# A four-layer gated cross-attention kernel: scales folded into the second weights on GpSimd, the last attention tile's normalization moved into the last stage

## The reference, cut to what matters

```python
x = x + tanh(g_xattn[0]) * L0_xattn(layernorm(x), ctx, ctx)        # stage A
x = x + tanh(g_ffn[0])   * L0_ffn(layernorm(x), ...)               # stage B
x = x + tanh(g_xattn[1]) * L1_xattn(layernorm(x), ctx, ...)        # queries, attention (C)
x = x + tanh(g_ffn[1])   * L1_ffn(layernorm(x), ...)               # stage D, causal attention
# L0_ffn, its end:
x = silu(x_gate) * x_up
x = fwht(x * SU_dp) / SCALE
x = x @ W_down.T * (Wscale_dp * SCALE)
```

## Time and profile before

| | |
|---|---|
| median of three runs | 2069.22 us (2066.19, 2069.22, 2069.27) |
| the profiled execution | 2064.52 us, its span 2062.8 us, mean granted TensorE clock 0.988 |
| TensorE busy | 1998.7 us (97%), weight loads 1677.0 us (81%) |
| VectorE busy | 1238.1 us (60%) |
| ScalarE busy | 1158.9 us (56%) |
| GpSimd busy | 826.3 us (40%) |
| DMA | 210.08 MB, mean 102 GB/s |

### The profile page before, as it was taken

How to read it: one execution, slowest core, us unless ns; L and a number is a source line. 1 busy time by engine, 2 the same in 40 slices (tenths; PEclk the granted TensorE clock), 3 DMA queues, 4 the chain that set the end, 5 groups by cost and what they waited for, 6 DMA issues and landing times. The chain is left out here.

```text
span 2062.8 us, 37477 instructions
## 1 busy us (share of the span) xinstructions
PE 1998.7 (97%) x13369; PEld 1677.0 (81%) x13369; DVE 1238.1 (60%) x2346; ACT 1158.9 (56%) x3064; POOL 826.3 (40%) x997
## 2 busy tenths in 40 slices
PE   8999999999999999999979998899999999899998
PEld 6877777777778888898868886799999999778886
DVE  6666666666644544564445555666666666466665
ACT  6666666666643333353333445877777777355544
POOL 3526436445321000000003445888888878022222
PEclk9999999999999999999989998999999999999999
DMA  6536346454364110203003434333333332311001
GB/s 185 155 93 193 121 132 206 119 154 140 104 246 166 62 61 1 72 1 118 1 26 107 122 117 148 91 95 98 115 100 110 93 112 88 116 59 54 28 28 37
DMA packets 193272, 210.08 MB, mean 102 GB/s; under 512 B 59533, under 2 KB 133757, under 8 KB 192589
## 3 DMA queue, kind: packets, MB, share of 16 engines
q1 hardware_dynamic: 193101, 207.83, 32.9%
HBM read 128.13 MB, written 79.66 MB: 101 GB/s over the span
## 5 line engine op out<-in xcount | busy, mean ns | idle before, releaser
L1864 POOL TENSOR_TENSOR qd_rows<-qd_rows,c_rsum 112x375 f32<-112x375 f32 x256 | 202.2, 811 | 85.5 <-DVE c_rsum L1994 78.3
L2000 DVE TENSOR_TENSOR c_pT_lo<-c_turned,c_pT_hi 125x336 fp32r<-125x336 f32 x256 | 128.4, 502 | 131.5 <-ACT c_pT_hi L1939 131.5
L1930 ACT ACTIVATE qd_rows<-c_score,c_nmax 112x375 f32<-112x375 f32 x256 | 147.1, 574 | 86.7 <-DVE c_nmax L1989 86.7
L1291 ACT ACTIVATE b_silu<-b_gate,ab_scales 128x512 f32<-128x512 f32 (+1 forms) x64 | 40.7, 636 | 252.8 <-PE b_up L1422 252.8
L1355 DVE SCALAR_TENSOR_TENSOR b_hidden<-b_up,ab_scales,b_silu 128x512 f32<-128x512 f32 (+1 forms) x64 | 43.7, 683 | 202.3 <-ACT b_silu L1291 202.3
L531 ACT ACTIVATE a_probs<-a_score,a_nmax 112x375 f32<-112x375 f32 x256 | 144.5, 575 | 2.6 <-DVE a_nmax L700 2.6
L2278 POOL TENSOR_TENSOR f_probs<-f_probs,f_rsum 112x448 f32<-112x448 f32 x64 | 59.7, 933 | 212.4 <-DVE f_rsum L2399 212.4
L953 PEld LDWEIGHTS a_turned<-keep_ident,a_probs 112*125 112x125 f32 x768 | 110.2, 188 | 35.4 <-issue 22.5
L1989 DVE TENSOR_REDUCE c_nmax<-c_score 112x1 f32<-112x375 f32 x256 | 137.4, 537 | 0.4 <-PE c_score L2070 0.4
L953 PE MATMUL a_turned<-keep_ident,a_probs 112*125 112x112 f32 x768 | 133.7, 283 | 1.0 <-DVE a_pT L706 0.7
L1269 POOL TENSOR_TENSOR ab_zT<-ab_zT,keep_ln_eps 128x1 f32<-128x1 f32 x1 | 0.2, 189 | 310.5 <-DVE ab_zT L1389 310.5
(11 more groups left out here) (347 smaller groups left out, 6074.7 us busy)
## 6 DMA issues: line engine op xcount, KB each, us to landing
q<-q_qT SPq DMA_DIRECT2D x14, 1024.0 KB
qd_raws<-q SPq DMA_DIRECT2D x64, 224.0 KB, 4.2
k<-bq_raw SPq DMA_DIRECT2D x16, 752.0 KB, 4.1
qd_raws<-k SPq DMA_DIRECT2D x64, 188.0 KB, 3.0
v<-bq_raw SPq DMA_DIRECT2D x48, 250.0 KB
qd_raws<-v SPq DMA_DIRECT2D x64, 187.5 KB
bq_raw<-in_ctx_dram SPq DMA_DIRECT2D x15, 672.0 KB
wug<-a_ug_turned SPq DMA_DIRECT2D x32, 256.0 KB, 2.3
```

What stands on the lines that cost most here:

```text
L1864: pool.tensor_tensor(probs[:, n % AHEAD, :], probs[:, n % AHEAD, :], rsum[:, n % (2 * H):n % (2 * H) + 1].broadcast_to([S, T]), ALU.mult). ...
L1930: act.activation(probs[:, n % AHEAD, :], score[n % AHEAD][0:S, 0:T], ACT.Exp, bias=nmax[:, c:c + 1], accum_out=sums[:, c:c + 1]).then_inc( ...
L2000: dve.tensor_tensor(pT[1][:, t % 2, :, j, :], src, f32(pT[0][:, t % 2, :, j, :]), ALU.subtract).then_inc(pT_split, 1)
```

## The change

It does three things.

First, `down_scale` is no longer multiplied into y. GpSimd multiplies it into each chunk's second weights in place, once, during the first group; ScalarE waits for it before it makes the chunk's high part in that group. The order on GpSimd is written out: chunks 0 and 1 before the addition L1251, chunk 2 after the deviation, 3 to 9 after the rotation, 10 to 15 after the head scales.

Second, statistics, deviation, normalize and the store of xn3 of the attention's last tile are done in the last stage. The two-tile buffers of both stages become one memory (`cd`), so that the tile stays where it is; the semaphores of the stores are handed over, and SP's wait for the stores moves to the last stage, in front of the loads of x3 and of later sequences.

Third, a projection of the last stage waits for the low part of x3 only before its second pass, and for the high part before its first.

```diff
@@ phase_b @@
         @block.gpsimd
         def _(pool):
+            def scale_down(c):
+                if c >= LEAD:
+                    pool.wait_ge(w_loaded[c], 32)
+                pool.tensor_tensor(down_chunk(c), down_chunk(c), down_scale[:, :], ALU.mult).then_inc(down_scaled, 1)
+
+            pool.wait_ge(scale_done, 1)
+            for c in range(LEAD):
+                scale_down(c)
             pool.wait_ge(ab["xres_loaded"], 16 * B)
...
+            scale_down(2)
             pool.wait_ge(z_done, 1)
...
+            for c in range(3, 10):
+                scale_down(c)
             pool.wait_ge(head_loaded, 32)
...
             pool.tensor_tensor(head_scale, head_clip, half, ALU.pow).then_inc(head_scaled, 1)
+            for c in range(10, IC):
+                scale_down(c)
...
+                if g == 0:
+                    act.wait_ge(down_scaled, c + 1)
                 act.activation(wd[0][:, p, :], down_chunk(c), ACT.Copy).then_inc(wd_hi, 1)
...
                     for k in range(TILES[g]):
                         dve.wait_ge(y_ready, first_tile[g] + k + 1)
-                        dve.tensor_tensor(y[k][:, :], y[k][:, :], down_scale[:, :], ALU.mult).then_inc(y_scaled, 1)
-                    for k in range(TILES[g]):
-                        dve.wait_ge(y_scaled, first_tile[g] + k + 1)
                         dve.tensor_tensor(xio[:, k, :], y[k][:, :], xio[:, k, :], ALU.add).then_inc(x_done, 1)
@@ phase_c_attention @@
-        xout = m.sb("xout", [P, 2, D])
-        xnorm = m.sb("xnorm", [P, 2, D])
+        xout, xnorm = cd["xout"], cd["xnorm"]
...
                 sp.dma_start(by_tiles(io["x3"])[i, :, :], xout[:, i % 2, :]).then_inc(x_stored[i % 2], 16)
+                if i == TILES - 1:
+                    return
                 sp.wait_ge(n_done, i + 1)
...
-            for i in range(2):
-                sp.wait_ge(x_stored[i], 16 * (TILES // 2))
-                sp.wait_ge(n_stored[i], 16 * (TILES // 2))
...
-                if i is not None:
+                if i is not None and i < TILES - 1:
                     deviations(i)
...
-                if i is not None:
+                if i is not None and i < TILES - 1:
                     moments(i)
...
-                if i is not None:
+                if i is not None and i < TILES - 1:
                     normalize(i)
@@ phase_d @@
-        xin = m.sb("xin", [S, 2, D])
-        xout = m.sb("xout", [S, 2, D])
+        xin, xout = cd["xnorm"][0:S, :, :], cd["xout"][0:S, :, :]
...
             load_weight("p")
+            sp.wait_ge(n_done, 1)
+            sp.dma_start(io["xn3"].rearrange("b s d -> (b s) d").rearrange("(t p) d -> t p d", p=P)[last_tile, :, :], tile_norm).then_inc(qd["n3_stored"][last_tile % 2], 16)
+            for i in range(2):
+                sp.wait_ge(qd["x3_stored"][i], 16 * (B * S // P // 2))
+                sp.wait_ge(qd["n3_stored"][i], 16 * (B * S // P // 2))
             for b in range(2):
                 load_residual(b)
...
+                if t == 1:
+                    pool.wait_ge(x_moments, 1)
+                    pool.tensor_tensor(x_ve[:, :], x_mv[:, 1:2], keep["ln_eps"][:, :], ALU.add).then_inc(x_shifted, 1)
+                    pool.wait_ge(x_shifted, 1)
+                    pool.tensor_tensor(x_rstd[:, :], x_ve[:, :], keep["neghalf"][:, 0:1], ALU.pow).then_inc(x_scaled, 1)
...
             weights_lo("v")
+            dve.bn_stats(x_bn[:, :], tile_out).then_inc(x_counted, 1)
+            dve.wait_ge(x_counted, 1)
+            dve.bn_aggr(x_mv[:, :], x_bn[:, :]).then_inc(x_moments, 1)
             for u in range(SLOTS + 3):
...
                 if u < WP_PARTS:
                     output_weights_lo(u)
+                if u == 0:
+                    dve.wait_ge(x_scaled, 1)
+                    dve.tensor_scalar(tile_norm, tile_out, x_mv[:, 0:1], x_rstd[:, 0:1], ALU.subtract, ALU.mult).then_inc(n_done, 1)
...
-                pe.wait_ge(work_lo, split_number(g, "x3"))
+                pe.wait_ge(work_hi, number(g, "x3"))
...
                 for m_, (s, r) in enumerate(PASSES):
+                    if m_ == 1:
+                        pe.wait_ge(work_lo, split_number(g, "x3"))
```

More of the change, by code:

```diff
@@ L1135, in phase_b @@
         xt_loaded = [m.sem(f"xt_loaded{g}") for g in range(GROUPS)]
-        x_loaded, x_done, y_ready, y_scaled = (m.sem(n) for n in ("x_loaded", "x_done", "y_ready", "y_scaled"))
+        x_loaded, x_done, y_ready, down_scaled = (m.sem(n) for n in ("x_loaded", "x_done", "y_ready", "down_scaled"))
         x_stored = bq["x2_stored"]
@@ L1398, in _ @@
                     dve.wait_ge(x_loaded, 16 * g + 16)
-                    dve.wait_ge(scale_done, 1)
                     for k in range(TILES[g]):
                         dve.wait_ge(y_ready, first_tile[g] + k + 1)
-                        dve.tensor_tensor(y[k][:, :], y[k][:, :], down_scale[:, :], ALU.mult).then_inc(y_scaled, 1)
-                    for k in range(TILES[g]):
-                        dve.wait_ge(y_scaled, first_tile[g] + k + 1)
                         dve.tensor_tensor(xio[:, k, :], y[k][:, :], xio[:, k, :], ALU.add).then_inc(x_done, 1)
@@ L1728, in _, with phase_c_attention @@
             batches(pe, head, body, TILES)
-def phase_c_attention(nc, keep, io, wo, qd):
+def phase_c_attention(nc, keep, io, wo, qd, cd):
     HEADS = B * H
@@ L1790, in phase_c_attention @@
         q_loaded, k_loaded, v_loaded = qd["q_loaded"], qd["k_loaded"], qd["v_loaded"]
-        x_loaded, x_stored, n_stored = ([m.sem(f"{n}{i}") for i in range(2)] for n in ("x_loaded", "x_stored", "n_stored"))
+        x_loaded = [m.sem(f"x_loaded{i}") for i in range(2)]
+        x_stored, n_stored = qd["x3_stored"], qd["n3_stored"]
         q_hi, q_split, k_hi, k_split, v_hi, v_split = (m.sem(n) for n in ("q_hi", "q_split", "k_hi", "k_split", "v_hi", "v_split"))
@@ L2118, in _, with phase_d @@
                     project((u - LAG) // 2)
-def phase_d(nc, keep, io, qd):
+def phase_d(nc, keep, io, qd, cd):
     SETS, RING, V_RING = 2, 4, 5
@@ L2194, in phase_d @@
         oT = [m.sb(f"oT_{n}", [P, DC, S], F32R) for n in ("hi", "lo")]
-        xin = m.sb("xin", [S, 2, D])
-        xout = m.sb("xout", [S, 2, D])
+        xin, xout = cd["xnorm"][0:S, :, :], cd["xout"][0:S, :, :]
+        last_tile = B * S // P - 1
+        tile_out, tile_norm = cd["xout"][:, last_tile % 2, :], cd["xnorm"][:, last_tile % 2, :]
+        stats = m.sb("stats", [P, 16])
+        x_bn, x_mv, x_ve, x_rstd = stats[:, 0:6], stats[:, 6:8], stats[:, 8:9], stats[:, 9:10]
+        x_counted, x_moments, x_shifted, x_scaled, n_done = (m.sem(n) for n in ("x_counted", "x_moments", "x_shifted", "x_scaled", "n_done"))
         score = m.ps("score", [P, 2 * SETS, 512])
@@ L2641, in flamingo_layers @@
             }
-            for name in ("q_loaded", "k_loaded", "v_loaded"):
+            for name in ("q_loaded", "k_loaded", "v_loaded", "x3_stored", "n3_stored"):
                 qd[name] = [m.sem(f"{name}{i}") for i in range(RAW)]
@@ L2647, in flamingo_layers @@
                 bq_scope.close()
-                phase_c_attention(nc, keep, io, wo, qd)
-            phase_d(nc, keep, io, qd)
+                cd_scope = ExitStack()
+                mcd = cd_scope.enter_context(Memory(nc, "cd"))
+                cd = {n: mcd.sb(n, [P, 2, D]) for n in ("xout", "xnorm")}
+                phase_c_attention(nc, keep, io, wo, qd, cd)
+            phase_d(nc, keep, io, qd, cd)
+            cd_scope.close()
 _INS = {"x": "x", "ctx": "ctx_2048", "g_xattn": "g_xattn", "g_ffn": "g_ffn"}
```

## The result

The changed kernel took 2053.48 us (median of four runs, 2052.05 to 2055.00), the kernel before beside it 2068.56 (four runs, 2066.19 to 2069.27): a ratio of 0.9929, 95% interval 0.9918 to 0.9941. The forecast was 2060.0 in a range of 2055.0 to 2064.5. The direction was right and the gain too small: 9.2 us forecast, 15.1 between these medians. The medians of two later measurements of the unaltered change say 13.9 (2053.70 against 2067.56) and 13.7 (2053.59 against 2067.31), with ratios of 0.9937 [0.9923, 0.9950] and 0.9934 [0.9921, 0.9948]. The two profiled executions lie 10.2 us apart, 2064.52 against 2054.35; part of what is missing there is 2.8 us that the changed kernel's execution lost ahead of the first product into y (stage A and B's first steps), in code that sets TensorE's pace in both kernels alike.

The account below looks back on a forecast made before the run. TensorE was taken to set the pace, so only places where it stands still could gain. Terms of 4.3 + 4.0 + 0.9 = 9.2 us, off the median of 2069.22, gave 2060.0 us, range 2055.0 to 2064.5.

Parts of the forecast that it names:

- B's scaling: Stage B: removing 14 multiplies of y by the scale from VectorE saves 4.3 us at group ends and B's end.
- The border: B's end to the queries: adds follow their tiles without multiplies, so the last store moves 2.3 us earlier.
- The first group's end: End of B's first group: TensorE's idle of 0.21 us goes.
- The second group's end: End of B's second group: TensorE's wait for hT_lo goes, 1.8 us saved, bounds 1.6 and 2.0.
- The border to the last stage: Attention's end: with the last tile's normalization moved out, the last stage starts 4.0 us earlier, bounds 2.4 and 4.0.
- First projection on the high parts: Last stage's start: first projection begins before x3's low part is done, saving 0.9 us, bounds 0.6 and 1.0.
- The clock: Rival, chance 0.12: shorter gaps keep TensorE at 2.4 GHz at the last stage's and queries' starts, 2 us each, 2056.0.
- the row at 593 speaks against it: Argument against the clock staying up: granted clock 0.90 after a gap of only about 2 us with thin work ahead.
- What is added: Sixteen GpSimd scalings in B's first group, 20.5 us, and work taken over by the last stage: cost 0, covered.
- the rival had named: GpSimd scalings block VectorE in B, tightest where it orders weights: half the price 2068.3 (chance 0.09), all 2076.6 (0.04).
- The reference point: The time the gain was taken off: the median of the runs shown of the kernel before, 2069.22 us.

Follow-up runs that it names:

- b_only: The kernel before with only the scaling of the second weights moved to GpSimd: 2061.29 us, ratio 0.9973.
- cd_only: The kernel before with only the attention's last-tile normalization moved into the last stage, projections still waiting for the low part first: 2061.24 us, ratio 0.997.
- lo_only: The kernel before with only the last stage's projection waits changed, high part before the first pass, low before the second: 2065.44 us, ratio 0.9990.
- fill_c: The kernel before, border length kept, with 20 matmuls that nothing reads behind the attention's last product: 2064.67 us, ratio 0.9990.
- after_wait: The changed kernel with SP's wait for the x3 stores' landing put back at the attention's end: 2057.15 us, ratio 0.9950.
- after_fill_a: The changed kernel with 1, 3 and 7 small matmuls that nothing reads in TensorE's idle places at stage A's end: 2051.59 us, ratio 0.9930.
- after_twice: The changed kernel with each chunk of the second weights scaled twice by GpSimd, result not the reference's: 2059.83 us, ratio to before 0.9960.
- after_fill_b: The changed kernel with 8 and 5 matmuls that nothing reads, between B and the queries and behind the queries' first transposes: 2052.51 us, ratio 0.9930.

## Why the prediction was right and wrong

**B's scaling**: forecast 4.3, measured 4.8 (b_only). The border gave 2.4 for 2.3. The first group's end gave 0.1 for 0.2, since the 0.21 in the earlier trace rows is an idle of the weight loads, which run beside the matmuls. The second group's end gave 2.2 for 1.8: 1.8 at its reduction, and then 0.4 more at the next projection, which no longer waited for the low weight part; the bounds, 1.6 and 2.0, were too tight.

**The border to the last stage**: forecast 4.0, its upper bound, measured 4.2 (cd_only). That nothing waits for a landing was right; the bare border, from the end of the last issue to the first instruction, took 1.02 us (1771.95 to 1772.97) where 1.25 had been taken from the border to the attention.

**First projection on the high parts**: forecast 0.9, measured 0.9 at 1.2 GHz (lo_only) and 1.2 in the change, where the clock was up (29.2 us from the first transpose to the first v against 30.5 in cd_only).

**The clock**: forecast 0, and given as a rival with 0.12. Here the prediction failed. The step was "the row at 593 speaks against it": a border with about the same idle, at which the clock falls, was taken to decide the one at 1773. The two differ in the work ahead. Windows of the changed kernel over the end of the attention and over the end of stage A (TensorE's busy time in the second number):

```profile
1765.00:1770.00 5.00, 5.00 (x24) 4.14 (x23) 1.08 (x2) 0.55 (x1) 0.00 (x0) 1.00 0.14 54
...
585.00:590.00 5.00, 4.66 (x24) 3.31 (x23) 3.26 (x6) 2.45 (x4) 0.00 (x0) 1.00 0.53 138
```

The attention ends in products without a gap; stage A has gaps here and two more, of 0.29 and 0.86 us, between 592 and 594. fill_c and cd_only show 2.7 us for the clock alone, and in after_wait, with 1.8 us more of border, it was lost. That the work ahead makes the difference between the two borders is argued from these rows; no run varied it by itself (after_fill_a filled the gaps and also shortened the last idle, to 1.26 us). Nor is it certain at the attention's end: in after_twice and after_fill_b the clock fell there behind the same border, and in such an execution the forecast's zero is right. The rival's price, 2 of up to 2.7 at each border, was somewhat low for the one; at the queries nothing came, where the idle is still 3.73 us and the clock fell.

**What is added**: forecast 0, and 0 it was; statistics, normalize, store and waits in the last stage left its later steps as they were. The cover holds for the scalings as they are, with 1.5 us to spare in the tightest step, and not for twice as many: doubled, they cost 4.8 us, at the place that the rival had named.

**The reference point**: the forecast was taken off the median of three runs, 2069.22. Over 48 runs in three later measurements the medians of the kernel before were 2066.90 to 2067.56. So of the miss of 6.5 us (2060.0 against 2053.48) some 1.9 belong to those three runs, 2.7 to the clock, 1.0 to the three mis-sized terms (0.5, 0.2 and 0.3), and the remaining 0.9 are within the spread of the runs.

## What to carry to other kernels

When an edit shortens a place where TensorE stands still, look at the granted clock behind that place: if it falls there, the shortening may be paid twice, once as idle and once as pace, and a handful of matmuls that nothing reads shows in one trace what the second part is worth. One border at which the clock falls does not decide another of the same length: look at the work ahead of it, and at more than one trace, since the clock need not do the same in each. And where an addition on GpSimd costs nothing, double it once: that shows how near the cover's edge is. Here the doubling cost 4.8 us, and the single scaling had 1.5 us to spare.

## What the runs showed of the hardware

- Behind the same stretch of code the clock falls in one trace and stays up in another: after an idle of 2.2 us behind dense work it stayed up five times in seven. That is worth 2.6 to 2.7 us. What decides between the two is not shown. At stage A's end it fell in all eleven traces without fillers there, but for a different time, so that the way from B's first instruction to the first y took 13.4 to 15.0 us (13.7, 14.9 and 14.9 in three traces of the same program).
- The last stage has such places of its own, in most traces near the first v and in two between 2000 and 2020 us; these two (fill_c, after_fill_b) took 223.4 and 223.3 us from the first to the last product with Wp, the others 220.3 to 221.8. How much of the 3 to 4 us between runs of one kernel is of this kind was not measured.
- A two-input operation of VectorE (128x512) and one of GpSimd that meet are both stretched, 0.69 to 1.78 and 1.28 to 2.27 us (the longest of the 13 scalings); the single-input copies among the weights' ordering were stretched too, to 2.56 us for two of 128x128 in after_twice (0.35 in the changed kernel at 672.70, behind the last scaling).
